# One decoder kernel: the gate's rounded `eu` rows are scaled back by GpSimd in place of ScalarE

## The reference

```python
x = x + _L0_ffn_ref(_layernorm(x), ...)      # routed feed-forward
x = x + _L1_attn_ref(_layernorm(x), ...)     # attention over the 4 batches at the same position
x = x + _L1_xattn_ref(_layernorm(x), ctx_2048)
x = x + _L1_ffn_ref(_layernorm(x), ...)      # ternary weights, 8-bit activations
```

```python
def quant_dequant_act_1x128(x):
    xb = x.reshape(E, M, K // BLK, BLK)
    amax = jnp.max(jnp.abs(xb), axis=-1, keepdims=True)
    safe = jnp.maximum(amax, ACT_EPS)
    q = (xb * (FP8_MAX / safe)).astype(jnp.float8_e4m3fn)
    return (q.astype(jnp.float32) * (safe / FP8_MAX)).reshape(E, M, K)
...
return jnp.einsum('emk,enk->emn', xq, wq)
```

## Time and profile before

| | |
|---|---|
| median of 3 runs | 1037.58 us (1036.24 to 1039.32) |
| the profiled execution | 1038.19 us |
| its span | 1036.3 us |
| instructions | 15017 |
| ACT L2250 in the span | 128 instructions, 40.7 us |

### The profile page before, as it was taken

One profiled execution on the slowest core, in us unless ns is written; L12 is line 12 of the kernel. 1 busy time (PEld: TensorE's weight loads), 2 busy tenths in 40 slices (PEclk: granted clock), 3 DMA queues, 4 the chain that ended last, 5 costly groups with the idle time before them and its releaser, 6 DMA issues.

```text
span 1036.3 us, 15017 instructions
## 1 busy us (share of the span) xinstructions
PE 1004.3 (97%) x4949; PEld 746.9 (72%) x4949; DVE 825.9 (80%) x1751; ACT 661.1 (64%) x1252; POOL 444.7 (43%) x655
## 2 busy tenths in 40 slices
PE   8999999999999999899999999998999999999998
PEld 7787788778877887665766887867766766666544
DVE  6898878787788787648898778677878988979875
ACT  5755555555555554356666567755489999898874
POOL 3435224422432233327888442016554645635520
PEclk9999999999999999899999999999999999999999
DMA  8453333333333422263100164310001111112124
GB/s 298 183 153 106 98 113 102 102 92 113 102 102 102 113 92 82 94 250 155 41 1 1 32 240 141 138 41 1 1 11 26 28 25 34 24 21 54 35 59 139
DMA packets 100860, 91.90 MB, mean 89 GB/s; under 512 B 79152, under 2 KB 80432, under 8 KB 96432
## 3 DMA queue, kind: packets, MB, share of 16 engines
q1 hardware_dynamic: 100784, 90.96, 28.0%
HBM read 56.69 MB, written 15.60 MB: 70 GB/s over the span
## 4 chain that ended last, share of the span: by engine, by line
PE 73%; DVE 12%; ACT 5%; issue 4%; POOL 4%; DMA 1%; SPq 0%; DVEq 0%; ACTq 0%; POOLq 0%
PE bank L471 56%; PE bank L555 5%; PE bank L943 3%; PE bank L479 3%; PE bank L546 1%; PE bank L566 1%; PE bank L485 1%; DMA land<-win_in 1%; DVE ctx_lo L1308 1%; DVE wgt L1066 1%; POOL prod L2633 1%; DVE spare L1347 1%; PE bank L855 1%; DVE half_lo L1421 0%; POOL y L2422 0%
## 5 line engine op out<-in xcount | busy, mean ns | idle before, releaser
L471 PE MATMUL bank<-win_hi,a_uT_hi 128*128 128x512 f32 (+1 forms) x320 | 126.1, 394 | 3.3 <-DVE win_lo L1023 2.5
L471 PE MATMUL bank<-win_lo,a_uT_hi 128*128 128x512 f32 (+1 forms) x320 | 120.5, 377 | 0.0
L471 PE MATMUL bank<-win_hi,a_uT_lo 128*128 128x512 f32 (+1 forms) x320 | 120.0, 375 | 0.0
L2422 POOL TENSOR_TENSOR y<-y,off 128x512 f32<-128x512 f32 x24 | 37.9, 1580 | 91.5 <-DVE off L1085 91.5
L471 PEld LDWEIGHTS bank<-win_hi,a_uT_hi 128*128 128x128 f32 x320 | 60.6, 189 | 17.0 <-DVE win_lo L1023 3.6
L471 PEld LDWEIGHTS bank<-win_hi,a_uT_lo 128*128 128x128 f32 x320 | 60.7, 190 | 11.3
L1066 DVE TENSOR_SCALAR wgt<-cum_all,neg 128x128 f32<-128x128 f32 x256 | 67.9, 328 | 0.4 <-DMA cum_all<-cum_rows 0.4
L1801 ACT ACTIVATE zs<-y 128x1024 uint16<-128x1024 uint16 x30 | 31.7, 1057 | 56.6 <-DVE y L1100 56.6
L471 PEld LDWEIGHTS bank<-win_lo,a_uT_hi 128*128 128x128 f32 x320 | 60.8, 190 | 9.5 <-issue 0.2
L471 PE MATMUL bank<-f,fqT_next 128*128 128x512 fp8e4 (+1 forms) x312 | 64.0, 362 | 0.0
L555 PEld LDWEIGHTS bank<-xs,wgt 128*128 128x128 f32 x512 | 61.3, 196 | 1.9 <-issue 0.4
(11 more groups left out here) (348 smaller groups left out, 3009.3 us busy)
## 6 DMA issues: line engine op xcount, KB each, us to landing
cum_all<-cum_rows SPq DMA_DIRECT2D x16, 1024.0 KB, 4.7
wchunk<-w_in SPq DMA_DIRECT2D x32, 256.0 KB, 5.6
y_rows<-zs SPq DMA_DIRECT2D x30, 256.0 KB, 2.0
stage<-f_in SPq DMA_DIRECT2D x3, 1408.0 KB, 6.0
x<-x_in SPq DMA_DIRECT2D x16, 256.0 KB, 5.5
land<-win_in SPq DMA_DIRECT2D x4, 1024.0 KB, 8.4
wq<-ctxT_in SPq DMA_DIRECT2D x4, 1024.0 KB, 6.6
out<-x SPq DMA_DIRECT2D x16, 256.0 KB, 2.6
```

The source lines that it names most:

```text
L471: made = e.matmul(bank, a, b, start=start and n == 0, stop=stop and n == len(pairs) - 1)
L2422: e.tensor_tensor(y[m % 2][:, cols], y[m % 2][:, cols], off[:], ALU.add).then_inc(sig("y_off"), 1)
```

## The change

The four ACT instructions that scale the rounded `eu` back go away, and four `tensor_scalar` on POOL take their place, with the same operands. On POOL they stand behind `h_gain` and ahead of `attend_begin`. POOL waits there for DVE's `e_fp8`, and, on its own engine, for `e_back` of the same tile, which it has issued a step earlier. The scaling by row 1 ahead of the rounding stays on ACT. `eu_ready`, for which PE's `turn_eu` and DVE's next `e_scales` wait, is now raised by POOL.

```diff
@@ scalar_program
             def scale_eu(n, row, ready, done):
                 u = eu[n % 2]
                 w.wait_ge(ready, n + 1)
-                if row == 2:
-                    w.wait_ge("e_fp8", n + 1)
                 for k in range(KD):
...
                     silu(t13, 1)
-                if t11 is not None:
-                    scale_eu(t11, 2, "e_back", "eu_ready")
                 if t10 is not None:
@@ gpsimd_program
+            def scale_back(n):
+                w.wait_ge("e_fp8", n + 1)
+                w.wait_ge("e_back", n + 1)
+                for k in range(KD):
+                    block = eu[n % 2][:, k * P:(k + 1) * P]
+                    made = e.tensor_scalar(block, block, am[:, 2, k:k + 1], 1.0, ALU.mult, ALU.mult)
+                made.then_inc(sig("eu_ready"), 1)
...
                 if t15 is not None:
                     h_gain(t15)
+                if t11 is not None:
+                    scale_back(t11)
                 if t9 is not None:
                     attend_begin(t9)
                     attend_part(t9, 2)
```

## The result

The changed kernel takes 1048.55 us (median; 1046.86 to 1052.59) against 1038.45 us for the kernel before on the same chip: a ratio of 1.0104, 95% interval 1.0079 to 1.0129, so it is slower, by 8 to 13 us. A second comparison on another chip (`after_again`) gave 1048.58 against 1037.18, 1.0107 (1.0089 to 1.0125). Predicted were 1046.0 us and a range of 1040 to 1054, which held. What the prediction put at 8.35 us is 10 to 11; the mechanism came out as told, one cost of the clock was not foreseen, and the split of the cost between its two causes was misread.

A forecast was written before the change was run, and what follows sets the result against it. PE and DVE were both taken as nearly full in the last stage's steps. Terms 1.1 + 2.9 + 2.75 + 0.25 + 1.35 = 8.35 us on 1038.2 profiled, less 0.6 to the median, gave 1046.0 us, range 1040 to 1054.

The forecast's parts named there:

- T: Delay of POOL's queue from the four added scalings: 1.3 us, bounds 1.0 and 2.2.
- up to 766: Last stage's steps to 766 us: PE gets `o` late at s = 3 (three earlier tiles attended to); 1.1 us.
- 785 to 841: One full round of four steps (s counts earlier tiles attended to): 0.4 at s = 1 plus 2.5, 2.9 us.
- 860 to 917: The next round of four steps: 0.25 plus 2.5, 2.75 us.
- the end: Last tiles: `o` late from POOL delays PE's transposition at s = 3 by 1.65, less 0.3 credit: 1.35 us.
- Step (b): `attend_begin` and later attention on POOL each T late; DVE waits at L1601, PE falls 0.85 us behind at s = 2.
- the 1.2 of `eu`: At s = 3 `eu` is ready at 826.26, not 825.03, with PE at its transposition at 825.18: about 1.2 us.
- the credit: Gain at the kernel's end from ACT's shorter queue, in PE's waits for ACT's copy `eT`: 0.3 us in all.
- rival 1: Only the direct lateness of `eu` counts, DVE's wait at L1601 is made up: 1041 us; chance 0.13.
- Rival 2: Not slower, through ACT's shorter queue at the end, at most 1.1 us gained: 1036.5 us; chance 0.04.
- Rival 4: The change does nothing, since PE bounds everything: 1037.6 us; chance 0.05.
- Rival 3: POOL dearer, locked out by DVE or at two-operand column rate: T = 1.7 to 2.2, 1049 to 1055 us; chance 0.18.

The follow-up runs named there:

- e5_half: The change, but ACT scales two of the four blocks back and POOL the other two: 1042.15 us, ratio 1.0037 to the kernel before.
- e1_dummy: Kernel before, `eu` still scaled on ACT, plus four scalings of another buffer at the change's place on POOL: 1046.74 us, ratio 1.0087.
- e9_act_late: Kernel before, with ACT's scaling back moved behind a square and the third SiLU, so only `eu` is later: 1043.14 us, ratio 1.0057.
- e8_warm: The change, with eight useless matmul calls on PE ahead of three transpositions of `eu`: 1046.47 us, ratio 1.0083 to the kernel before.
- e4_no_back: Scaling back left out altogether, `eu` goes to PE unscaled: 1036.68 us, ratio 0.9996 to the kernel before.
- e3_begin_first: The change, with `attend_begin` ahead of the four scalings on POOL: 1058.58 us, ratio 1.0195 to the kernel before.
- e6_add_later: The change, with DVE's first addition L1601 behind the third piece of the gate: 1047.53 us, ratio 1.0099 to the kernel before.
- e7_before_add_later: Kernel before, scaling on ACT, with DVE's first addition behind the third piece of the gate: 1038.16 us, ratio 1.0001.

## Why the prediction was right, and where not

| step of the prediction | predicted | measured in the trace |
|---|---|---|
| T, four scalings in POOL's queue | 1.3 | 1.38 |
| DVE's wait at L1601 | 1.2 | 1.24 to 1.25 at s = 1, 2, 3 (1.01 the first time) |
| up to 766 | 1.1 | 1.3 |
| 785 to 841 | 2.9 | 3.2 |
| 860 to 917 | 2.75 | 3.2 |
| 936, s = 1 | 0.25 | 0.44 |
| the end | 1.35 | 2.5, of it some 0.7 the clock |
| the clock, behind s = 3 at 911 | 0 | 1.56 |
| sum | 8.35 | 12.3 in the profiled execution |

**The mechanism held.** The price of an operation that the trace did not show, built from three neighbours (base, pointer, columns), was 5% off. By the 1.8 cycles an element of the Trainium skill (GPSIMD Engine Reference, 3.1 Elementwise) T would have been about 1.7, an estimate; the trace has 1.38. The same section also has 1.03 cycles an element, for its shortest loop bodies, and does not say which figure holds for this operation; the trace is near the 1.03. The reserve that I read at s = 2 and 3 (none) and the two places of T on the way were right: with T at 1.38 in the same sum the rounds would be 3.1 and 2.9, within 0.3 us of the measured 3.2. `e5_half` shows the same at half the size. The period of four steps, forecast at 78.3, is 79.0 (831.83 to 910.81). It was said to start from 75.5, four steps of 18.88; it was 75.8 already (825.18 to 900.95), since before the change too the step from s = 2 to 3 took PE longer than 18.9.

**What was misplaced.** Step (b) had PE lose 0.85 at s = 2 behind L1606. In the change PE waits 0.58 for `eu` there (forecast 0.3), and what is left behind L1606 is 0.19. The 0.85 appears where `eu` is not late, in `e1_dummy`. What PE loses up to s = 2 is set by the later of the two, and it is about the same either way, so the sum did not notice. At s = 3 the two terms, T on POOL's place and the 1.2 of `eu`, do follow each other on one chain, and there adding them was right. What was wrong is the reading made of this later, in the expectation of `e1_dummy`, that each cause alone is worth about half. In the prediction's own walk the late `eu` alone was 3.9 us less the credit (rival 1); `e9_act_late` has 6.0, and 4.8 in the trace.

**The end.** I had PE wait for `o` at s = 3, 1.65 us late. It didn't: `o` was transposed without a wait at 995.60, since PE had already waited 1.38 for `eu` and lost another 1.7 in the products behind it. L1601 beside `pv` takes 1.52 there, forecast 1.45; that step was right, but in this trace it is not the one that sets the end. Where the clock stays up it is: in `e8_warm` PE does wait for `o`, 0.65 us at 989.40, and the last three tiles cost 1.8 us in place of the change's 2.5. So of the 1.4 us of that spell only some 0.7 were added to the end; the forecast was 1.35.

```profile
989.96 1.52 DVE L1601 TENSOR_TENSOR o<-o,pv 128x512 f32<-128x512 f32 x1
...
990.40 5.36 PE L471 MATMUL bank<-wq,eT 128*128 128x512 f32 x8 [0.78 <-ACT eT L2195]
995.60 0.60 PE L479 MATMUL bank<-ident,o 128*128 128x128 f32 x4
```

In `e8_warm`:

```profile
989.40 0.63 PE L479 MATMUL bank<-ident,o 128*128 128x128 f32 x4 [0.65 <-POOL o L2660]
```

**Slips in the working.** The bounds of T treat the overlap of 0.04 us unlike the forecast: with it the lower is 4 x 0.22 = 0.9 and not 1.0, the upper 4 x 0.52 = 2.1 and not 2.2. The 0.4 at s = 1 of the first round has no working; the reading used at 861 gives 0.3 there (786.49 + 1.36 against 787.58), and 0.5 was measured. None of these moves the forecast by more than 0.1 us.

**The size.** Rival 1 (only the direct lateness, 1041) falls: DVE's wait is not made up, and `e1_dummy`, in which ACT scales `eu` where it always did and POOL's queue alone is longer, is 9.2 us slower. Rival 2 (ACT's shorter queue wins) falls with `e4_no_back`. Rival 4 falls with the result. Rival 3's size, T = 1.7 to 2.2, is not reached in the change; but its mechanism exists, and `e3_begin_first` shows it. What the forecast lacked is in the main the clock: 1.56 us behind 911 and some 0.7 at the end, 2.3 of the 4 us that the trace has above 8.35. The rest is spread: 0.2 to 0.45 in each of the steps of the table, T among them. In the medians (10.1 and 11.4) the sum is 1.8 to 3 us too low, which the range of 14 us took in.

What stays open: why the medians (10.1 and 11.4) are 2.2 and 0.7 us below the lateness in the two traces of the change, 12.3 and 12.1. The part ahead of the stage is one place where it can lie: in the traces shown here the stage begins from 3.1 us earlier to 2.3 us later than in the trace of before, without any change there. Another is the clock: the four runs of the change on the first chip scatter by 5.7 us, at granted clocks of 0.992 to 0.997.

## What to carry to other kernels

Before work goes to an idler engine, look at what stands behind its place in that engine's queue, and follow it round until it comes back to the same queue: where such a loop (here from POOL over DVE to POOL, 19.96 us in one step of four) is longer than the busiest engine's own step (18.9), what is put into it is lost (0.69 and 1.38 us were tried), once for each time that the chain passes it, though that engine is busy for 43% only. And price the relief by leaving the work out: here that alone showed that at most 2 us were to be won. Two delays that meet at the same waiting engine are compared, not added.

## What the runs showed of the hardware

**The clock after a wait.** Behind the waits of 1.88 and 1.38 us PE ran slower for about 4 us. The matmuls of 128x384 after 910.81:

```profile
911.63 0.34 PE L471 MATMUL bank<-wqkv_hi,d_uT_lo 128*128 128x384 f32 x1
911.81 0.45 PE L471 MATMUL bank<-wqkv_hi,d_uT_hi 128*128 128x384 f32 x1
912.06 0.52 PE L471 MATMUL bank<-wqkv_lo,d_uT_hi 128*128 128x384 f32 x1
912.38 0.52 PE L471 MATMUL bank<-wqkv_hi,d_uT_lo 128*128 128x384 f32 x1
...
914.62 0.93 PE L479 MATMUL bank<-ident,d_u 128*128 128x128 f32 x4
```

0.52 us in place of 0.34, and starts 0.32 apart in place of 0.17: the lower level, 1.2 GHz. Across the two spells PE's lateness grew by 1.56 and 1.40 us, about as much as the waits ahead of them lasted. It isn't the wait's length alone: behind the 1.85 us at 831.83 the clock stayed at 1.00, and in `e3_begin_first` it stayed at 1.00 behind 2.00 and 1.92 us and fell to 0.83 behind 1.90 and 1.87; in `e6_add_later` it stayed at 1.00 behind 1.86, twice. The same two places fell in both traces of the change. Nor is it bound to the change: the trace of `e7_before_add_later` has such a spell between 970 and 985 us, behind waits of 0.78 and 1.08, and six others have one at about 725 us. In five of these six no other follows. What else decides was not tried. The windows of `e3_begin_first`:

```profile
790.00:800.00 10.00, 8.26 (x31) 6.24 (x32) 7.09 (x14) 5.16 (x8) 4.79 (x9) 0.83 0.07 13
810.00:820.00 10.00, 8.00 (x38) 5.88 (x38) 8.11 (x19) 6.60 (x12) 6.89 (x15) 1.00 0.07 14
830.00:840.00 10.00, 8.08 (x43) 6.38 (x41) 8.11 (x19) 6.91 (x12) 9.12 (x17) 1.00 0.15 30
995.00:1005.00 10.00, 8.57 (x28) 4.08 (x28) 7.07 (x15) 5.98 (x11) 6.26 (x11) 0.83 0.07 13
```

**One operation, two prices.** The four scalings take 1.42 us in the change at every s, where DVE runs the gate L1669, with one input in SBUF, beside them and then waits. In `e3_begin_first` they take 1.84 where DVE's L1601, with two, runs beside them, and the longest single one takes 0.935 us in place of 0.385. So the price of an operation on POOL hangs on the DVE instruction beside it. The other side shows as well: L1601 is 1.52 us beside POOL's `pv` product and 0.68 where no POOL product runs.

The Trainium skill (SBUF — State Buffer, Who interferes with whom) says that a VectorE instruction with two SBUF inputs and a GpSimd instruction that reads SBUF contend for one shared read interface, and that one with at most one SBUF input does not, unless it runs in a two-port mode. The prediction left out this last condition, which does not touch L1669. These numbers agree with the page.
